# Sums over 64 nodes from 104 rows on either side of a middle row, in the two column halves of TensorE's array

## The reference

```python
h = jnp.maximum(_layernorm(x, axis=-1), 0.0)
W_rel = jnp.einsum('rb,bdf->rdf', w_comp, weight)           # 32 relations from 8 bases
seg = etype * n_nodes + dst
agg = jax.ops.segment_sum(h[src] * norm, seg, num_segments=n_rels * n_nodes)
node_repr = jnp.einsum('rnd,rdf->nf', agg.reshape(n_rels, n_nodes, d_in), W_rel)
out = x + jax.nn.relu(node_repr + h_bias + h @ loop_weight)
```

## Time and profile before

| | |
|---|---|
| median of three runs | 1066.85 us |
| the profiled execution | 1066.05 us |
| its span, first to last instruction | 1064.3 us |
| PE busy | 1043.9 us (98%) |
| DVE busy | 1018.1 us (96%) |
| ACT busy | 925.4 us (87%) |
| POOL busy | 805.2 us (76%) |
| DMA | 150.97 MB, mean 142 GB/s |

### The profile page before, as it was taken

One profiled execution on the slowest core, in us unless ns is written; L12 is line 12 of the kernel. 1 busy time (PEld: TensorE's weight loads), 2 busy tenths in 40 slices (PEclk: granted clock), 3 DMA queues, 4 the chain that ended last, 5 costly groups with the idle time before them and its releaser, 6 DMA issues. The chain is left out here.

```text
span 1064.3 us, 23588 instructions
## 1 busy us (share of the span) xinstructions
PE 1043.9 (98%) x4903; PEld 664.6 (62%) x4903; DVE 1018.1 (96%) x4370; ACT 925.4 (87%) x3252; POOL 805.2 (76%) x1381
## 2 busy tenths in 40 slices
PE   5999999999999999999999999999999999999997
PEld 2444444444444444444444444444899999999997
DVE  6999999999999999999999999999999999999995
ACT  6999999999999999999999999999588888888884
POOL 7888888888888888888888888886555555555553
PEclk9999999999999999999999999999999999999999
DMA  4323232323232444222232323222599999999993
GB/s 105 94 77 83 76 101 69 93 66 103 66 94 73 125 116 134 77 81 83 76 88 72 93 76 85 75 66 80 173 300 298 297 297 299 295 295 301 296 299 96
DMA packets 91092, 150.97 MB, mean 142 GB/s; under 512 B 18578, under 2 KB 57826, under 8 KB 90946
## 3 DMA queue, kind: packets, MB, share of 16 engines
q0 software_dynamic: 28224, 76.93, 26.0%
q1 hardware_dynamic: 61250, 71.78, 22.0%
q10 hardware_dynamic: 1472, 0.74, 0.3%
HBM read 97.88 MB, written 51.49 MB: 140 GB/s over the span
## 5 line engine op out<-in xcount | busy, mean ns | idle before, releaser
L463 POOL DMA_INDIRECT xg<-x,idx x392 | 389.8, 994 | 75.3 <-issue 49.0
L704 PE MATMUL y_ps<-w_all,hT 128*128 128x512 f32 x784 | 401.7, 594 | 0.7 <-issue 0.7
L710 PE MATMUL y_ps<-w_all,hT 128*128 128x512 f32 x784 | 400.5, 592 | 0.0
L559 ACT ACTIVATE z<-y_ps,mix 128x128 f32<-128x128 f32 x784 | 245.0, 364 | 56.9 <-PE y_ps L710 37.2
L710 PEld LDWEIGHTS y_ps<-w_all,hT 128*128 128x128 f32 x784 | 148.9, 190 | 188.4 <-issue 182.7
L892 DVE SCALAR_TENSOR_TENSOR sum_b<-y_ps,mix,sum_b 128x128 f32<-128x128 f32 x784 | 265.3, 338 | 0.0
L704 PEld LDWEIGHTS y_ps<-w_all,hT 128*128 128x128 f32 x784 | 141.3, 191 | 141.1 <-issue 122.4
L416 POOL TENSOR_TENSOR u<-z 128x128 f32<-128x128 f32 x392 | 181.8, 464 | 36.4 <-ACT z L559 28.1
L512 POOL DMA_DIRECT2D out<-res x98 | 76.1, 777 | 133.0 <-DVE res L1131 133.0
L587 ACT ACTIVATE hw<-xw,shift,nrstd 128x128 f32<-128x128 f32 x392 | 162.7, 482 | 1.7
L777 PE MATMUL y_ps<-w_loop,hwT 128*128 128x128 f32 x782 | 151.1, 274 | 0.0
(11 more groups left out here) (95 smaller groups left out, 1406.2 us busy)
## 6 DMA issues: line engine op xcount, KB each, us to landing
seg<-msgs SPq DMA_DIRECT2D x391, 96.8 KB
msgs<-msg SPq DMA_DIRECT2D x98, 258.0 KB
xw<-x POOLq DMA_DIRECT2D x97, 256.0 KB, 5.1
out<-res POOLq DMA_DIRECT2D x97, 256.0 KB, 4.3
type_bc<-type_rows SPq DMA_DIRECT2D x56, 112.0 KB
xg<-x,idx POOLq DMA_INDIRECT x392
w_all<-weight ACTq DMA_DIRECT2D x1, 512.0 KB
dst_i<-dst ACTq DMA_DIRECT2D x1, 196.0 KB, 3.3
```

The lines of the kernel that those rows point to most:

```text
L463: nc.gpsimd.indirect_dma_start(xg[:, q, j, :], None, x, bass.IndirectOffsetOnAxis(ap=idx[:, q, j:j + 1], axis=0)).then_inc(s_gather[q * G ...
L559: ins = nc.scalar.activation(z[:, r, b, :], y_ps[r][:, b, :], ACT.Copy, scale=mix[:, q, j, b:b + 1])
L704: nc.tensor.matmul(y_ps[r][:, B // 2:B, :], hT[:, q, j, :], w_all[:, B // 2:B, :], start=True, stop=True).then_inc(s_y_high, 1)
L710: nc.tensor.matmul(y_ps[r][:, 0:B // 2, :], hT[:, q, j, :], w_all[:, 0:B // 2, :], start=True, stop=True).then_inc(s_y, 1)
```

## The change

Each window of 128 nodes becomes two halves of 64 nodes. What was a table of first rows is now a table of middle rows: the row at which the messages of the second half begin. From it 104 rows on either side are loaded, 208 a window, the upper 104 for the first half and the lower 104 for the second.

- `load_windows`: partition p gets row p of the first half and row p of the second: two pieces of 516 bytes on each of 104 partitions, where it was one of 1032 on each of 96. A block of 128 rows (zeros, node number -1) stands ahead of the messages, so that the first window can reach back.
- `picks`: 104 partitions x 8 x 64 elements. `relative` subtracts from each half its own first node (`half_off`).
- `window_sums`: first the four products with the loop weight, then for each window two products of 105 rows x 64 columns, which write partitions 0 to 63 and 64 to 127 of the same sums. Both have a bias row.
- `store_results` moves from POOL to SP, ahead of the loads of group g; POOL keeps the wait for the results of g-8 and the load of x.
- The check for windows with too many edges becomes one for halves: is the edge 104 further on in the same 64 nodes (`dst_far`, one more input of 196 KB). It adds operations of 128 x 392 elements to `row_step`, a matmul and a copy at group 18 (`CROWD_STEP`). 50000 edges of the reference's own input put at most 92 on any 64 nodes, so the slow path is not taken.
- At the start, the indices of the first two groups are loaded by a transfer of their own (`FIRST`), and the first four sums of pairs of POOL are placed a little earlier. `bin_limits` has one small operation more.

```diff
-CHUNKS = 2
+HALVES = 2
+FIRST = 8
-SEG_P = 96
+HALF = P // 2
+SEG_P = 104
@@ sync
-            sp.dma_start(src_all[:, :], src).then_inc(s_src, 16)
+            sp.dma_start(src_all[:, 0:FIRST], src[:, 0:FIRST]).then_inc(s_src_first, 16)
+            sp.dma_start(src_all[:, FIRST:NT], src[:, FIRST:NT]).then_inc(s_src, 16)
...
+            sp.dma_start(dst_far_i[:, :], dst_far).then_inc(s_far, 16)
...
                 for j, row in enumerate(rows):
-                    sp.dma_start(seg[0:SEG_P, q, j, :, :].rearrange("p c f -> p (c f)"),
-                                 msgs[bass.ds(row, SEG), :].rearrange("(p c) f -> p (c f)", c=CHUNKS)
+                    sp.dma_start(seg[0:SEG_P, q, j, :, :],
+                                 msgs[bass.ds(row, SEG), :].rearrange("(c p) f -> p c f", c=HALVES)
                                  ).then_inc(done, 16)
...
+            def store_results(g, q, full=G, last=0):
+                r = q % NRING
+                sp.wait_ge(n_res, g + 1)
+                if full:
+                    sp.dma_start(OUT_WIN[:, bass.ds(g * G, full), :], res[:, r, 0:full, :]).then_inc(n_out[r], 16)
...
             def reload_windows(g, n, q, full=G, last=0):
-                sp.wait_ge(n_res, g - (LRING - 1))
+                store_results(g - LRING, q)
                 load_windows(g, q, row_tab, n_seg[q], full, last)
@@ gpsimd
             def load_x(g, n, q, full=G, last=0):
-                store_results(g - LRING, q)
+                pool.wait_ge(n_res, g - LRING + 1)
@@ tensor
+                if g == CROWD_STEP:
+                    pe.wait_ge(s_crowded, 1)
+                    nc.tensor.matmul(mix_ps[0:1, 0:1], ones16[:, :], crowded16[:, :], start=True, stop=True)
...
                 for j in range(windows):
-                    y = win_ps[r][:, j, :]
-                    nc.tensor.matmul(y, hwT[:, r, j, :], w_loop[:, :], start=True, stop=False)
-                    nc.tensor.matmul(y, pick[:, r, j, 0, :][0:SEG_P], seg[0:SEG_P, q, j, 0, 0:F],
-                                     start=False, stop=False)
-                    mm = nc.tensor.matmul(y, pick[:, r, j, 1, :][0:SEG_P + 1], seg[0:SEG_P + 1, q, j, 1, 0:F],
-                                          start=False, stop=True)
+                    nc.tensor.matmul(win_ps[r][:, j, :], hwT[:, r, j, :], w_loop[:, :], start=j == 0, stop=False)
+                for j in range(windows):
+                    for c in range(HALVES):
+                        mm = nc.tensor.matmul(win_ps[r][:, j, :][c * HALF:(c + 1) * HALF],
+                                              pick[:, r, j, c, :][0:SEG_P + 1], seg[0:SEG_P + 1, q, j, c, 0:F],
+                                              start=False, stop=j == windows - 1)
@@ vector
             def picks(r, first, windows):
-                shape = [SEG_P, (windows - first) * CHUNKS, P]
+                shape = [SEG_P, (windows - first) * HALVES, HALF]
...
-                    iota_n[0:SEG_P, :].unsqueeze(1).to_broadcast(shape),
+                    iota_n[0:SEG_P, 0:HALF].unsqueeze(1).to_broadcast(shape),
```

More of the change, by code:

```diff
@@ L45 @@
 SPAN = 8
+CROWD_STEP = 18
 ROW_STEPS = 8
@@ L88, in pad_node, with build_layer @@
     return -(-nodes // P) * P
-def build_layer(nc, x, src, dst_cols, dst, dst_next, type_rows, norm, weight, mix_weight, loop_weight, bias, out):
+def build_layer(nc, x, src, dst_cols, dst, dst_next, type_rows, norm, dst_far, weight, mix_weight, loop_weight, bias, out):
     N, D = x.shape
@@ L207, in build_layer @@
         hwT = sb("hwT", [P, NRING, G, P])
[L208 to L210 removed]
+        seg = sb("seg", [P, LRING, G, HALVES, C])
+        rel = sb("rel", [SEG_P, NRING, G, HALVES])
+        pick = sb("pick", [P, NRING, G, HALVES, HALF])
         res = sb("res", [P, NRING, G, F])
@@ L357, in load_windows @@
                     table[0:1, bass.ds(g * G, windows)], (mybir.EngineType.SP,), min_val=0, max_val=ROWS - SEG,
-                    skip_runtime_bounds_check_because="first_row is clamped to EP - SEG or counts compacted rows")
+                    skip_runtime_bounds_check_because="a window's row is clamped to the edges' rows or counts compacted rows")
                 for j, row in enumerate(rows):
-                    sp.dma_start(seg[0:SEG_P, q, j, :, :].rearrange("p c f -> p (c f)"),
-                                 msgs[bass.ds(row, SEG), :].rearrange("(p c) f -> p (c f)", c=CHUNKS)
+                    sp.dma_start(seg[0:SEG_P, q, j, :, :],
+                                 msgs[bass.ds(row, SEG), :].rearrange("(c p) f -> p c f", c=HALVES)
                                  ).then_inc(done, 16)
@@ L395, in _ @@
                     load_windows(q, q, row_tab, c_reload)
+            def store_results(g, q, full=G, last=0):
[3 more added lines that the diff above has]
+                    sp.dma_start(OUT_WIN[:, bass.ds(g * G, full), :], res[:, r, 0:full, :]).then_inc(n_out[r], 16)
+                if last:
+                    sp.dma_start(out[(NW - 1) * P:N, :], res[0:last, r, full, :]).then_inc(n_out[r], 16)
             def reload_windows(g, n, q, full=G, last=0):
-                sp.wait_ge(n_res, g - (LRING - 1))
+                store_results(g - LRING, q)
                 load_windows(g, q, row_tab, n_seg[q], full, last)
             sweep(sp, NGW - 1, reload_windows, LRING, LRING, LRING)
-            g = NGW - 1
-            reload_windows(g, g // LRING, g % LRING, LAST_FULL, LAST)
+            last_g = NGW - 1
+            reload_windows(last_g, last_g // LRING, last_g % LRING, LAST_FULL, LAST)
+            for g in range(NGW - LRING, last_g):
+                store_results(g, g % NRING)
+            store_results(last_g, last_g % NRING, LAST_FULL, LAST)
+            for r in range(NRING):
+                sp.wait_ge(n_out[r], 16 * (len(range(r, NGW, NRING)) + (r == last_g % NRING and LAST_FULL > 0)))
         @block.gpsimd
@@ L461, in gathers @@
                 for j in range(G):
+                    if g == 2 and j == G - 1:
+                        add_pair(0, 0)
                     if not beyond(g, NG):
@@ L467, in gathers @@
                         gains(g - 2, (q - 2) % RING)
-                    if not is_before(g, 3):
+                    if g == 3 and j < G - 1:
+                        add_pair(j + 1, (j + 1) % RING)
+                    if not is_before(g, 4):
                         add_pair(g * G + (j - 3 * G), (q * G + j) % RING)
@@ L1188 @@
     dst_next[0:P - 1, 0] = dst[1:P, 0]
+    dst_far = np.full((P * tiles,), -1, dst.dtype)
+    dst_far[0:inputs["dst"].size - SEG_P] = inputs["dst"].reshape(-1)[SEG_P:]
     w_comp = inputs["L0_gnn_w_comp"]
@@ L1200 @@
     give("norm", group_cols("edge_weight1", 0))
+    give("dst_far", dst_far.reshape(P, tiles))
     give("weight", inputs["L0_gnn_weight"])
```

137 lines of the change are left out of this document (80 added, 57 removed).

## The result

The changed kernel takes 1091.53 us (median of 4 runs, 1089.45 to 1093.78) beside 1066.89 for the kernel before on the same chip (4 runs, 1066.74 to 1068.96): ratio 1.0224, 95% interval 1.0204 to 1.0245. It is slower by 24.6 us; 1093 was predicted. The time is right, but not every step behind it is: two wrong ones cancel, and that the forecast came within 1.5 us is luck.

A forecast was written before the change was run, and what follows sets the result against it. PE set the pace before, at 3.12 us a group; after the change the DMA engines would bind at 3.56, so 770.1 + 90 T gives 1090.5 us, plus 1.75 around the span and 0.8 to the median: 1093 us, range 1050 to 1136.

The forecast's parts named there:

- PE's part: Window stage: half products run side by side, PE's need falls from 3.12 to 2.23 us a group, worth at most 17.6 us.
- ACT's ring: Window stage: ACT's relu-to-relu cycle of relus, hand-over, transposes and copy, unchanged, a floor of 2.94 us a group.
- rival 3: PE, window stage: halves not side by side, shape changes drain at most 0.17 us each; 1100 us; chance 0.06 with rival 4.
- DVE: Window stage: `pick` about half of 1.20 us, DVE falls from 3.02 to about 2.45 us a group, no bound.
- The prices of the pieces: DMA, window stage: 33 ns per 516-byte load piece, 31 per 512-byte store piece; 57.0 engine-us a group in all.
- 3.56 us on 16 engines: DMA, window stage: 57.0 engine-us a group spread over 16 engines set the period at 3.56 us, bounds 3.15 to 3.94.
- rival 2: Window loads: 104 partitions use only 13 engines, 3.95 us a group, 1128 us, total DMA share 0.85 to 0.93; chance 0.31.
- rival 1: DMA, window stage: engines' share is elastic, small packets cost their bytes; 1056 us, or 1049 if DMA binds nothing; chance 0.22.
- SP: SP's queue, window stage: 2.47 us of work a group plus one issue of 0.32 us gives 2.8 us.
- rival 4: SP's issuing becomes the bound, two-piece issues 0.1 us longer: 3.2 us a group, 1075 us; chance 0.06 with rival 3.
- Stores on SP: SP's queue, window stage: the store's wait delays nobody; loads come 0.3 to 0.45 us later, with groups of cover.
- From period to time: Whole kernel: start of loads at 757.7, 90 periods T and a 12.4 us tail give a span of 770.1 + 90 T.

The follow-up runs named there:

- experiment 5: Changed kernel with 96 partitions, two neighbouring rows in one 1032-byte piece (sums wrong): 1054.17 us with stores on SP, 1048.27 us with stores on POOL.
- experiment 6: Changed kernel, window reloads bringing only one of each partition's two pieces, same number of SP instructions: 1061.39 us, ratio 0.9952 to the kernel before.
- experiment 3: Kernel before, without halves, with 104 and 112 partitions instead of 96: 1065.67 us and 1065.20 us.
- experiment 4: Stores back on POOL in the changed kernel, 1093.72 us, and with 96 partitions, 1066.38 us; kernel before with stores moved to SP, 1065.64 us.

## Why the prediction was right, step by step

A chain of kernels that differ in one thing each after its first step, by medians, puts the 24.6 us together:

| from | to | us |
|---|---|---|
| before, 1066.9 | halves, pieces of 1032, 96 partitions, stores on POOL, 1048.3 | -18.6 |
| | pieces of 516, 1066.4 | +18.1 |
| | 104 partitions, 1093.7 | +27.3 |
| | stores on SP, and the kernel is the one after, 1091.5 | -2.2 |

112 partitions stand at 1086.6, so, with 96 to 112 rows at 20.2 us, 8 rows are about 10 of the 27.3 us, and 17 are due to 104 itself. (Medians from different chips differ by up to 3 us for the kernel before; by the ratios the terms are the same within 1.5.)

- **PE's part: right.** Side by side, and worth 18.6 us where 17.6 was said to be the most; ACT's ring binds at 2.94. PE's need was mis-sized, 2.51 us for 2.23: the two changes of shape with the steps behind them, 0.28, of which rival 3 had spoken at up to 0.17 each. All other steps are within 2 ns of what they were. The Trainium skill, "TensorEngine Tiling (Array Packing)", section Tiling Modes, has such a drain; 92 ns at once, some 140 with the step behind it, is what the change costs here.
- **DVE: right.** `pick` 0.69 us for 1.20, DVE 140.81/57 = 2.47 us a group for 2.45 predicted.
- **The prices of the pieces: right in the sum.** In the trace after, 47293 packets of 516 bytes in q1 last 32.5 ns on average (33 taken), 29107 of 512 bytes 28.8 (31 taken). By the queues' shares, (0.754 + 0.254) x 16 x 200 / 57 = 56.6 engine-us a group, and 57.0 with the 0.4 of instructions: the predicted sum. In it x came out dearer (14.1 plus its reports for 13.2) and the stores cheaper (14.8 for 15.9). That pieces and not bytes count is shown by experiment 5. The Trainium skill, "DMA: Bandwidth & Descriptors", section Specifications, has the full rate from 512 bytes on; here 516 bytes in 32.5 ns are 15.9 GB/s, 1032 in 58.0 (experiment 5, stores on SP) 17.8, and the kernel felt it.
- **"3.56 us on 16 engines": the step that failed, twice.** First, the loads go to 13 engines; that is rival 2's mechanism, held less likely at 0.31. On each of the 13 a group leaves 64 x 32.5 ns of loads, 32 x 28.8 of stores, 64 x 219.6/16 of x (a packet of 4096 bytes lasted 219.6) and some 0.08 of reports and instructions: 3.96 us, if loads are spread evenly over them. Second, an engine's records may overlap, so that its share goes over 1: rival 1's mechanism. 3.96/3.52 = 1.12 on the 13; the same sum gives 1.11 with 104 partitions and the stores on POOL, and with 96 and 112 partitions the share of all 16 was 1.10 and 1.12. So too many engine-us on too few engines, over a share of 1.12 that the forecast had at 1.0, came out where 57.0/16 = 3.56 did, by accident. Rival 2's time was too long by the overlap, rival 1's too short because no run went over 1.12. On the three other engines it leaves 1.83/3.52 = 0.52, and (13 x 1.12 + 3 x 0.52)/16 = 1.01 is the row's own mean, as it must be: the trace has no row for a single engine, so 1.12 is worked out and not read. The sign that I gave for rival 2, a share of 0.85 to 0.93, was wrong for the same reason, and would have denied what was there.
- **SP: under-sized.** 2.8 us predicted, 3.2 as rival 4. It works 3.19 with 104 partitions (experiment 6): rival 4's size, and it is not hidden: it held experiment 6, and in the kernel after SP has next to no wait either. But rival 4's reason was wrong: an issue with two pieces a partition takes no longer (0.31 us at least, before 0.32). What was missed is that SP waited in 51 of 64 groups only (33.3 us of 800 to 1000, so 0.52 a group and not 0.65, and 2.60 us of work), that the store costs 0.42 and not 0.32, and the 0.19 by which the read of the table got longer: 3.21.
- **Stores on SP: next to nothing, as said** (-2.2 and -1.4 us with 104 partitions and in the kernel before, +2.2 with 96; the last is clear of the noise by the ratios).
- **From period to time: right.** 770.1 + 90 x 3.52 = 1086.9 for a span of 1087.6. The first load is issued at 757.88, it was 757.67; the last issue follows `res` by 1.0 us, it was 1.9:

```profile
1084.49 0.56 DVE L1177 SCALAR_TENSOR_TENSOR res<-y_ps,xw 128x384 f32<-128x384 f32 x1 [0.98 <-PE y_ps L807]
1085.49 0.47 SPq L422 DMA_DIRECT2D out<-res  x1
```

- **Edge stage and start: nothing, as taken:** the first load of the window stage comes 0.2 us later.

What stays open: how the 17 us of 104 partitions split between three idle engines and a second thing found beside it, below. For the engines speaks experiment 3, where the loads landed late by themselves; in the kernel after the last landing comes 5.5 us after the start of the fourth issue, no later than with 112 or 96 partitions (5.7 and 5.3), and its SP issues were held up no more (0.5 us a group over their least times, 0.6 with 112), which speaks for SP. Open too is whether SP or the 13 engines end last in the kernel after group by group, since each stretches the other. A version with 1032-byte pieces that keeps the rows of the halves apart was not found: neighbouring rows belong to the same half. Of the kernels that leave nothing out, the one before with its stores on SP is the fastest, by 0.2%, which is what can just be told.

## What to carry to other kernels

Count pieces and engines, not bytes: before widening a transfer, see by which number up to 16 its partitions divide, and what its smallest run of bytes is; here 96, 104 and 112 rows took 1066, 1094 and 1087 us (stores on POOL). 104 need not cost anything: in the kernel before, with pieces of 1032 bytes and loads in time, it cost nothing. A queue that never waits is either the bound or held by what stands behind it; take work from it (experiment 4) and from what is behind it (experiment 6) to see which. When a forecast comes out right, take its parts one at a time in experiments: this one came within 1.5 us by luck, with the likeliest case's mechanism wrong in two places.

## What the runs showed of the hardware

- A DMA share over 1.0 is possible: with the loads late it stood at 1.09 to 1.12 in the four kernels with 516-byte pieces on all 16 engines, and at 1.04 with 318 GB/s and nothing late.
- After loads of 104 partitions SP's read of the table took 0.49 us in the median, after loads of 96 or 112 0.30. In the kernel after with the stores on POOL it was 0.57 and 0.30, in the kernel before 0.46 and 0.30. First the kernel after, then 112 partitions, then experiment 6 (ns, min/median/max):

```profile
L374 SPq TENSOR_LOAD <-row_tab x57: 483/492/814, 800.3 to 997.6; - x57
```

```profile
L374 SPq TENSOR_LOAD <-row_tab x59: 293/301/312, 800.8 to 999.2; - x59
```

```profile
L374 SPq TENSOR_LOAD <-row_tab x63: 482/491/546, 800.8 to 998.3; - x63
```

  Half the pieces change nothing, the 104 does. Another trace of it: the loads' semaphore gets its first count 0.5 us after the start of the issue with 104 partitions, long before data lands, and 2.3 to 3.2 us after it with 96 or 112. It is 0.19 us of a queue that never waits, so it may hold up to 90 x 0.19 = 17 us of the kernel after; that easing SP by 0.62 us gave only 0.04 (experiment 4) speaks against it, and no run took this alone away.
- The last landing of a group's loads came 9.0 us after the start of the fourth issue with 104 partitions of 1032-byte pieces, 5.4 with 112 and 4.5 with 96, on a queue that had waits left.
- Two products in different column halves start 6 to 11 ns apart, and a change between full and half shape costs PE 92 ns, some 140 with the step behind it.
